# Edge messages in laps of twelve slots, one slot picked by TensorE, and plain early fetches in the update

## The reference

```python
h = relu(layernorm(x))
msg_input = concat([h[src], edge_sh, edge_radial], axis=-1)      # 200000 x 81
m = silu(silu(msg_input @ W1 + b1) @ W2 + b2) @ W3 + b3          # 200000 x 64
agg = segment_sum(m, dst, 6250)
u_in = concat([h, agg], axis=-1)
gate = sigmoid(u_in @ G + gb)
u = silu(layernorm(u_in @ U1 + ub1))
x = x + h + gate * layernorm(u @ U2 + ub2)
```

## Time and profile before

| | |
|---|---|
| median of 3 runs | 3172.85 us (3168.97 to 3183.3) |
| the profiled execution | 3195.68 us, span 3194.0 us |
| PE busy, share of the span | 2752.0 us, 86% |
| POOL busy | 1515.6 us, 47% |
| DVE busy | 1919.2 us, 60% |
| ACT busy | 1613.8 us, 51% |

### The profile page before, as it was taken

How to read it: one execution, slowest core, us unless ns; L and a number is a source line. 1 busy time by engine, 2 the same in 40 slices (tenths; PEclk the granted TensorE clock), 3 DMA queues, 4 the chain that set the end, 5 groups by cost and what they waited for, 6 DMA issues and landing times.

```text
span 3194.0 us, 63519 instructions
## 1 busy us (share of the span) xinstructions
PE 2752.0 (86%) x20761; PEld 2179.8 (68%) x20761; DVE 1919.2 (60%) x2346; ACT 1613.8 (51%) x2994; POOL 1515.6 (47%) x1572
## 2 busy tenths in 40 slices
PE   4499999967999985889888989888989898898975
PEld 3377777757998982666666666666767666676654
DVE  5899999964444564455555555555555555555526
ACT  2488888832332223455545555545555554555534
POOL 4000000000000006777777777777777777777765
PEclk9999999968999996899999999999999999999976
DMA  3133333326998973445444445544445555444421
GB/s 109 61 141 161 141 161 141 161 121 260 365 361 320 359 287 79 107 121 132 120 119 119 122 117 125 129 121 121 121 117 125 119 128 124 120 121 116 126 48 30
DMA packets 216659, 477.09 MB, mean 149 GB/s; under 512 B 53932, under 2 KB 114910, under 8 KB 197601
## 3 DMA queue, kind: packets, MB, share of 16 engines
q1 hardware_dynamic: 159976, 422.33, 38.5%
q0 software_dynamic: 55632, 52.47, 10.3%
q10 hardware_dynamic: 1001, 1.66, 0.1%
HBM read 339.87 MB, written 136.41 MB: 149 GB/s over the span
## 4 chain that ended last, share of the span: by engine, by line
PE 47%; POOL 25%; issue 11%; DVE 11%; DMA 4%; ACT 1%; DVEq 0%; POOLq 0%; ACTq 0%
POOL arena L663 22%; PE ps L791 14%; PE ps L961 8%; PE ps L810 6%; PE ps L973 5%; PE ps L980 5%; PE ps L988 5%; DMA arena<-m_tab,m_idx 3%; DVE arena L1868 2%; POOL ybuf L678 2%; PE ps L950 2%; DVE stageT L1844 2%; PE ps L706 1%; PE ps L694 1%; POOL arena L604 0%
## 5 line engine op out<-in xcount | busy, mean ns | idle before, releaser
L663 POOL DMA_INDIRECT arena<-m_tab,m_idx x1463 | 1391.4, 951 | 1586.0 <-issue 1574.8
L2118 DVE TENSOR_TENSOR_SCAN arena<-arena,ps 128x512 f32<-128x512 f32 x391 | 500.2, 1279 | 856.6 <-ACT ps L1335 723.4
L988 PEld LDWEIGHTS ps<-weights,arena 128*128 128x128 f32 x3128 | 438.2, 203 | 210.3 <-issue 196.4
L1330 ACT ACTIVATE arena<-ps,weights 128x512 f32<-128x512 f32 x391 | 268.7, 687 | 490.7 <-PE ps L973 483.1
L791 PE MATMUL ps<-arena 128*128 128x195 bf16 (+1 forms) x4802 | 481.5, 248 | 32.2 <-DVE arena L1810 31.6
L791 PEld LDWEIGHTS ps<-arena 128*128 128x128 f16 x4802 | 416.8, 98 | 62.8 <-DVE arena L1810 31.8
L961 PE MATMUL ps<-ends,arena 128*128 128x192 bf16 x4900 | 458.9, 252 | 0.0
L973 PE MATMUL ps<-arena,weights 81*128 81x512 f32 x782 | 443.5, 651 | 0.0
L980 PE MATMUL ps<-arena,weights 128*128 128x512 f32 x782 | 435.9, 640 | 0.0
L961 PEld LDWEIGHTS ps<-ends,arena 128*128 128x128 bf16 x4900 | 421.7, 100 | 7.0
L988 PE MATMUL ps<-weights,arena 128*128 128x64 f32 x3128 | 415.4, 279 | 1.7 <-ACT arena L1342 1.7
(11 more groups left out here) (269 smaller groups left out, 2294.1 us busy)
## 6 DMA issues: line engine op xcount, KB each, us to landing
arena<-count_d SPq DMA_DIRECT2D x98, 1568.0 KB, 8.5
arena<-keep_d SPq DMA_DIRECT2D x391, 256.0 KB, 3.9
count_d<-arena SPq DMA_DIRECT2D x49, 1568.0 KB, 5.1
scan_rows<-arena SPq DMA_DIRECT2D x391, 128.0 KB
arena<-m_tab,m_idx POOLq DMA_INDIRECT x1463, 3.3
arena<-attr_in SPq DMA_DIRECT2D x391, 34.0 KB
arena<-src_row SPq DMA_DIRECT2D x25, 258.0 KB
hT_d<-stageT ACTq DMA_DIRECT2D x12, 132.0 KB
```

The costliest lines, as they stand in the source:

```text
L663: pool.indirect_dma_start(m_rows[:, k, t, :], None, m_tab, bass.IndirectOffsetOnAxis(ap=m_idx[:, k, t:t + 1].bitcast(U32), axis=0))\
L988: last = pe.matmul(m_back[k % BACK_RING][:, t * D:(t + 1) * D], m_scan[:, k % SCAN_RING, t * P:(t + 1) * P], W("W3"), start=True, stop=True)
L2118: dve.tensor_tensor_scan(m_scan[:, k % SCAN_RING, :], m_mask[:, k % MASK_RING, :], m_term[k % TERM_RING], before, ALU.mult, ALU.add).then_ ...
```

## The change

- `LOOP` becomes 12: `LAPS` 33, the loop runs 31 laps, the last lap has 7 slots (`LAST`). The rings follow: `m_rows` 12 slots, masks 6 for 5, and attributes, scans and outputs 4 for 5; indices are copied four slots at a time.
- One slot in twelve is picked. Its 9 groups are multiplied in slots 5 to 9, two in each of slots 5 to 8 (`PICKS_AT`). The marks are made three after scan 0 and two after each of scans 1, 2 and 3 (`MARKS_AT`). The parts are joined before scan 7 (`JOIN_AT`).
- The fetches of the update are plain indirect DMAs without an add. They no longer wait for all stores: each group waits until the stores that hold its nodes' last edges are done (`slots_needed`, read into a register by POOL, against the count of `out_ready`). DVE adds degree times b3 (`add_b3`) and the residual `xres`; POOL no longer computes in the update. PE waits for DVE's `agg_ready` where it waited for the DMAs.
- The last four `rows_back` get PSUM banks of their own (`last_back`), and the 32 `keep_busy` matmuls write bank 0.
- SP clears the last 20 slots' rows of `scan_rows` by a DMA of 256-byte rows at the start.

```diff
-LOOP = 15
+LOOP = 12
-MASK_RING = 5
-ATTR_RING, TERM_RING, SCAN_RING, OUT_RING = 5, 3, 5, 5
+MASK_RING = 6
+ATTR_RING, TERM_RING, SCAN_RING, OUT_RING = 4, 3, 4, 4
+CLEARED = 20
-IDX_STEP = 5
+IDX_STEP = 4
-PICK_RING, PICK_BLOCKS, PICK_LAG = 3, 6, 5
+PICK_RING, PICK_BLOCKS = 3, 6
+PICKS_AT = {5: (0, 1), 6: (2, 3), 7: (4, 5), 8: (6, 7), 9: (8,)}
+MARKS_AT = {0: (0, 1, 2), 1: (3, 4), 2: (5, 6), 3: (7, 8)}
+JOIN_AT = 7
 ...
+        last_back = [ps[:, 2 + TERM_RING + k % 3, 0:TB * D] for k in range(LAG)]
 ...
+        fetch_slots = [*range(LAST, PICKED), *range(1, 1 + len(END_GROUPS) - (PICKED - LAST))]
+        rows_fetched = [e1.gathered[k] for k in fetch_slots]
+        fetched = [DMA * TB * (LAPS if k < LAST else LAPS - 1) for k in fetch_slots]
 ...
             sp.wait_ge(masks_stored, 6 * DMA)
+            sp.dma_start(scan_rows[(NSLOT - CLEARED) * BE:NSLOT * BE, :], zero_row[:, :].unsqueeze(1).to_broadcast([1, CLEARED * BE, D]))\
+              .then_inc(zero_stored, DMA)
 ...
+            for k in range(OUT_RING):
+                sp.wait_ge(e1.stored[k], DMA * ((NSLOT - k + OUT_RING - 1) // OUT_RING))
+            sp.sem_inc(e1.out_ready, OUT_RING)
             for i, (a, n) in enumerate(END_GROUPS):
                 sp.wait_ge(y_ready, i + 1)
 ...
-            for k in range(OUT_RING):
-                pool.wait_ge(e1.stored[k], DMA * ((NSLOT - k + OUT_RING - 1) // OUT_RING))
             for i, (a, n) in enumerate(END_GROUPS):
+                needed = slots_needed[P - 1:P, a + n - 1:a + n]
+                pool.wait_ge(e1.turn_done, LOOP * (LAPS - 1) + fetch_slots[i] + 1 + (LOOP if fetch_slots[i] < LAST else 0))
+                pool.wait_ge(e1.out_ready, pool.to_reg(pool.value_load(needed, min_val=OUT_RING + 1, max_val=NSLOT + OUT_RING)))
+                pool.sem_inc(alone, 1)
                 for j in range(a, a + n):
                     pool.indirect_dma_start(ybuf[:, j, :], None, scan_rows,
-                                            bass.IndirectOffsetOnAxis(ap=end_idx[:, j:j + 1].bitcast(U32), axis=0),
-                                            compute_op=ALU.add).then_inc(rows_fetched[i], DMA)
-            for i, (a, n) in enumerate(END_GROUPS):
-                pool.wait_ge(let_in, i + 1)
-                pool.tensor_tensor(xres[:, a:a + n, :], xres[:, a:a + n, :], ybuf[:, a:a + n, :], ALU.add).then_inc(y_ready, 1)
+                                            bass.IndirectOffsetOnAxis(ap=end_idx[:, j:j + 1].bitcast(U32), axis=0))\
+                        .then_inc(rows_fetched[i], DMA)
 ...
-                    if PICK_LAG <= k < PICK_LAG + len(PICKS):
-                        pick_rows(i, k - PICK_LAG)
+                    for n in PICKS_AT.get(k, ()):
+                        pick_rows(i, n)
 ...
-                pe.wait_ge(rows_fetched[i], FETCHED + n * DMA)
+                pe.wait_ge(agg_ready, i + 1)
 ...
-            keep_busy(6, 32)
+            keep_busy(0, 32)
 ...
+                link(dve.tensor_scalar(mean[:, :], end_f[:, :], BE - 1.0, float(BE), ALU.add, ALU.max))
+                link(dve.tensor_copy(slots_needed[:, :], mean[:, :]))
+                link(dve.tensor_scalar(slots_needed[:, :], slots_needed[:, :], BE.bit_length() - 1, None, ALU.logical_shift_right))
+                link(dve.tensor_scalar(slots_needed[:, :], slots_needed[:, :], OUT_RING, None, ALU.add))
 ...
-                    link(dve.tensor_tensor(ybuf[:, :, :], per_node(deg_one[:, :, 0], D), per_feature(V("b3"), J), ALU.mult))
+                    link(dve.tensor_tensor(hbuf[:, :, :], per_node(deg_one[:, :, 0], D), per_feature(V("b3"), J), ALU.mult))
 ...
-                    if k < len(PICKS):
-                        mark_pick(i, k)
+                    for n in MARKS_AT.get(k, ()):
+                        mark_pick(i, n)
 ...
+            def add_b3(i, a, n):
+
+                dve.wait_ge(rows_fetched[i], fetched[i] + n * DMA)
+                dve.tensor_tensor(ybuf[:, a:a + n, :], ybuf[:, a:a + n, :], hbuf[:, a:a + n, :], ALU.add).then_inc(agg_ready, 1)
 ...
-                dve.scalar_tensor_tensor(v, of_rows[:, a:a + n, HID:ROW], 1.0, v, ALU.add, ALU.mult).then_inc(let_in, 1)
+                link(dve.scalar_tensor_tensor(v, of_rows[:, a:a + n, HID:ROW], 1.0, v, ALU.add, ALU.mult))
+                dve.tensor_tensor(xres[:, a:a + n, :], xres[:, a:a + n, :], v, ALU.add).then_inc(y_ready, 1)
```

More of the change, by code:

```diff
@@ L397, in late_block @@
             return first % RING, first // RING + k + 1, first + RING * k
-        update_ready, hT_stored, hT_loaded, let_in = (sem(n) for n in ("update_ready", "hT_stored", "hT_loaded", "let_in"))
+        update_ready, hT_stored, hT_loaded, agg_ready = (sem(n) for n in ("update_ready", "hT_stored", "hT_loaded", "agg_ready"))
         agg_turned, agg_copied, agg_multiplied = (sem(n) for n in ("agg_turned", "agg_copied", "agg_multiplied"))
-        rows_fetched = e1.gathered[1:1 + len(END_GROUPS)]
-        FETCHED = DMA * TB * (LAPS - 1)
+        fetch_slots = [*range(LAST, PICKED), *range(1, 1 + len(END_GROUPS) - (PICKED - LAST))]
+        rows_fetched = [e1.gathered[k] for k in fetch_slots]
+        fetched = [DMA * TB * (LAPS if k < LAST else LAPS - 1) for k in fetch_slots]
         u_ready, u_squared, u_staged, u_turned, u_done, gate_done, v_done, v_added, v_squared = (sem(n) for n in (
@@ L563, in move_slot @@
                     load_mask(s - LAG + MASK_RING, (k - LAG) % MASK_RING)
+            sp.wait_ge(zero_stored, 2 * DMA)
             for k in range(LOOP):
@@ L980, in hidden_out, with rows_back @@
                 pe.matmul(m_term[k % TERM_RING], W("W2"), m_hid[:, k % HID_RING, :], start=True, stop=True).then_inc(e1.w2_done, 1)
-            def rows_back(s, k, late):
+            def rows_back(s, k, late, to=m_back[0], ring=BACK_RING):
                 pe.wait_ge(e1.scan_done, s + 1)
                 if late:
-                    pe.wait_ge(e1.out_ready, s - BACK_RING + 1)
+                    pe.wait_ge(e1.out_ready, s - ring + 1)
                 for t in range(TB):
-                    last = pe.matmul(m_back[k % BACK_RING][:, t * D:(t + 1) * D], m_scan[:, k % SCAN_RING, t * P:(t + 1) * P], W("W3"),
+                    last = pe.matmul(to[:, t * D:(t + 1) * D], m_scan[:, k % SCAN_RING, t * P:(t + 1) * P], W("W3"),
                                      start=True, stop=True)
@@ L1018, in _ @@
                 hidden_out(s, s % LOOP, True)
-            for s in range(NSLOT - LAG, NSLOT):
-                rows_back(s, s % LOOP, True)
+            for n, s in enumerate(range(NSLOT - LAG, NSLOT)):
+                rows_back(s, s % LOOP, True, last_back[n], n + 1 if n < 3 else 3)
             flat = ones[:, :].bitcast(BF16)
@@ L1335, in second_silu, with rows_out @@
                 act.activation(m_term[k % TERM_RING], m_term[k % TERM_RING], ACT.Silu, bias=W("b2")).then_inc(e1.silu2_done, 1)
-            def rows_out(s, k, lap):
+            def rows_out(s, k, lap, of=m_back[0]):
                 act.wait_ge(e1.back_done, s + 1)
@@ L1341, in rows_out @@
                     act.wait_ge(e1.stored[k % OUT_RING], DMA * ((LOOP // OUT_RING) * lap + k // OUT_RING))
-                act.activation(m_out[:, k % OUT_RING, :, :].rearrange("p t f -> p (t f)"), m_back[k % BACK_RING], ACT.Copy)\
+                act.activation(m_out[:, k % OUT_RING, :, :].rearrange("p t f -> p (t f)"), of, ACT.Copy)\
                    .then_inc(e1.out_ready, 1)
@@ L1368, in _ @@
                 second_silu(s, s % LOOP)
-            for s in range(NSLOT - LAG, NSLOT):
-                rows_out(s, s % LOOP, s // LOOP)
+            for n, s in enumerate(range(NSLOT - LAG, NSLOT)):
+                rows_out(s, s % LOOP, s // LOOP, last_back[n])
             def square_u(i, a, n):
@@ L2135, in _ @@
                         know_pick(i)
-                    if k == PICK_LAG + len(PICKS) - 3:
+                    if k == JOIN_AT:
                         join_parts(i)
@@ L2205, in let_through @@
                 dve.wait_ge(gate_done, i + 1)
-                dve.scalar_tensor_tensor(v, of_rows[:, a:a + n, HID:ROW], 1.0, v, ALU.add, ALU.mult).then_inc(let_in, 1)
+                link(dve.scalar_tensor_tensor(v, of_rows[:, a:a + n, HID:ROW], 1.0, v, ALU.add, ALU.mult))
+                dve.tensor_tensor(xres[:, a:a + n, :], xres[:, a:a + n, :], v, ALU.add).then_inc(y_ready, 1)
             for i, (a, n) in enumerate(END_GROUPS):
                 v = i - 2 if i >= 2 else None
+                if i == 0:
+                    add_b3(i, a, n)
+                if i + 1 < len(END_GROUPS):
+                    add_b3(i + 1, *END_GROUPS[i + 1])
                 add_update_bias(i, a, n)
```

2 lines of the change are left out of this document (1 added, 1 removed).

## The result

The changed kernel takes 3141.5 us (median of 7 runs, 3124.8 to 3156.7), the kernel before in the same comparison 3186.1 (7 runs, 3169.0 to 3195.2): ratio 0.988, interval 0.985 to 0.991. It is faster by 37 us by the ratio and by 45 by the two medians; against the median of three runs that the forecast started from, 3172.85, it is 31. Forecast were 62. The time of 3141.5 lies 31 us above the predicted one, inside the range.

The account below looks back on a forecast made before the run. POOL's gather issue, 1.256 us per DMA, was taken as the bound. Laps -30, small DVE instructions +1, start -16, pace -16, pickless last lap -1 made -62 from 3172.85: 3110.9 us, range 3094 to 3148.

Parts of the forecast that it names:

- The laps: Message block: 24 fewer gather DMAs at POOL's 1.256 us each, 30 us faster; 1 us more from the pickless last lap.
- The slack of 5.2 us per lap: Message block: PE needs 49.8 us per new lap at full clock against POOL's 55.0.
- Rivals 1 and 2: Message block: 1, PE takes over as bound, 3150 us, chance 0.13; 2, DVE's mark ring stalls PE, 3238 us, 0.09.
- DVE's stall for the sources: Laps: DVE waits 5.3 us for the sources' load before shift, scan and marks; costed at nothing, margin 5 us.
- The rule of the Trainium skill: Laps: VectorE in a two-port mode blocks GpSimd's DMA descriptors; marks would cost up to 89 us, left out of the sum.
- The clearing DMA: Program start, SP's queue: clearing 10240 rows of 256 bytes costs between 0 and 5 us, taken as 0.
- The end: From the last gather to the program's end: start -16 us, pace -16 us, drain 0.
- Start: Update, up to stage step of group 0: 3075.1 instead of 3091.0, -16 us, bounds -17 to -13.
- Pace: Update, stage steps of groups 0 to 8: 69 us instead of 84.9, -16 us, bounds -20 to -5.
- Drain: After the last stage step: 18.1 us stays, POOL's last add replaced by one on DVE, 0 change.
- The early fetches: Update: plain fetches follow the last gather at 1.25 us each; register read per group 0 to 3 us, taken as hidden.
- Rival 3: Update: early fetches don't come early, or PE at half clock; the end gives 18 us instead of 32, 3125 us, chance 0.14.

Follow-up runs that it names:

- the laps alone: Kernel before with laps of twelve and their rings, marks and picks, old end, no clearing DMA: 3139.1 us, ratio 0.986; on a slower chip 4424.2 us, 1.012.
- the cheap clear: Changed kernel with the clear done from a tile of zeros in 1280 rows of 2048 bytes: 3104.0 us, 0.976 against the kernel before; slower chip 1.016.

## Why the prediction came out as it did

- *The laps: right.* -32 us where -30 and -1 stood; POOL at 1.255 us per gather, no waits of note, slots 5 to 8 at 6.77 us. The slack of 5.2 us per lap was 4.7 when measured. Rivals 1 and 2 fall: POOL waited 8.2 us for PE in the whole kernel, and DVE's marks, though they waited 188 us for PE, were in time. DVE's stall for the sources, where I left a margin of 5 us, came to 26.9 us in 30 laps and passed on to no other engine. Nor did the marks hold up POOL: 279 of them at 1.82 us, and gathers that take 944 ns in the median and come every 1.255 us. The rule of the Trainium skill (SBUF — State Buffer, the "DVE blocks DMA" trap), by which they would have if they ran in a two-port mode, finds nothing for it in this trace either; which mode they run in no view shows.
- *The clearing DMA: wrong, and this is the step that failed.* "No row shows its price: between 0 and 5 us, I take 0." It cost 45.5 us alone, and 52.1 in the changed kernel. I had counted who needs SP's queue (nobody for 60 us) but not how long the DMA itself lasts; at 11.0 ns for each of 10240 rows it is 113 us, and it ends 52.6 us after the first count store is issued. "PE and DVE carry the counting there" was the reason for the zero, and it doesn't hold: both stand still from 160 to 180 us, since the counting can't go on before its first store has landed. The bounds were too narrow as well: with no row for a DMA of 10240 small rows, the 0 to 5 us were a guess at the issue time, and not a bound on the transfer. The rival that belongs here (the queue blocked, the counting waits) was missing.
- *The end: the mechanism right, three terms too small.* The first two came out beyond their bounds, the third had none. Start -21.9 for -16: from the first turn to stage 0 it took 3068.19 - 3059.04 = 9.2 us (11.5 taken, 10 to 14.8 as bounds), the idle matmuls took 4.4 for 6.0, at the full clock, and the last scan ended 11.6 us after the last gather, for 13.5 before. W3's products ended 1 us after it, as said. Pace -25.3 for -16: I took 9.0 us per group because that lay near rows with PE at a low clock, though I had DVE's own sum of 8.3 as the lower bound. DVE's sum was the pace (8.07, and 6.5 to 7.1 for the first two gaps, with less work behind them). Drain -6.4 for 0: DVE's last steps take as long as before (9.6 for 9.9 us), but from DVE's last step to the end 8.2 us passed before, and 2.1 now. The add is not the reason: on POOL it began 0.1 us after DVE's last step and took 0.6, and SP issued the last store at once, as now. 5.5 of the 6.1 us are the shorter wait of SP for PE's sequencer at the end of the program (5.7 before, 3.6 with the laps alone, 0.2 in every kernel with the new end). Which part of the new end does it was not tried; the forecast took the drain over from before and didn't ask what it was made of.
- *The early fetches: right.* They follow 1.25 us behind the last gather, at 1.25 us each, and the register reads cost nothing that shows (all 14.9 us of idle time in front of 49 of them is the 0.3 each of any indirect DMA). Rival 3 falls: the early start alone gives 13 us.
- *The sum.* Two errors of opposite sign: +52 for the clear, -22 for the end. -62 + 52 - 22 = -32; the traces, without the 14 of the start and the 7 of the level between the counting and the gathers, have -54.5 + 14 + 7 = -33.5. The medians, -31 to -45 according to which are compared, mix these levels. That the time lies inside the range is thus in part luck: the end gave back what the clear took beyond it. With the cheap clear the forecast's own sum of -62 would have been too small by 20 us.

## What to carry to other kernels

A DMA that nobody waits for still has a length: look for what one of its rows costs (here 11.0 ns for 256 bytes, 113 us in all, where the same bytes took 7 us in longer rows from more partitions), and ask who stands behind it in the queue when it is still running. Where two engines are about equally loaded in a pipelined stage, take the busiest one's sum of work as the pace, not a value between the bounds. And a trade of DMA issues for matmuls wins only while PE has slack: on a chip that feeds PE late the laps alone lose 1.2%, and the changed kernel with the cheap clear 1.6%.

## What the runs showed of the hardware that I had not expected

- A DMA that spreads one row of zeros over 10240 rows of 256 bytes in HBM moves 24 GB/s (11.0 ns per row), and a later DMA on its queue took 41.3 us to issue. The same bytes in 1280 rows of 2048, from 128 partitions, were gone in 7 us, at 380 to 390 GB/s.
- POOL's issue period is 1.25 us for a plain indirect DMA of 128 rows, whether the rows come from the node table or from the stored scans, and 1.88 for the adding form.
- At the end of the program SP waited 5.7 us for PE's sequencer in the kernel before, though PE's last matmuls began at 3178.9 and the span ends at 3194.0, and 0.2 us in the changed one.
- The first 76 us of the same code take 61 us in other runs. PE makes the difference: from 44 us on a group of 14 matmuls (64x64, f32) takes 3.25 us in the one and 1.77 in the other, though the granted clock of the stretch from 45 to 60 us reads 1.00 in both. Beyond that, 9 us come and go between the last count store and the first gather.
- Where PE's instructions came late, the chips ran every version slower, the kernel before by 37 to 40%.
